# A four-layer graph network on one core: last weights turned by VectorE from blocks, the attention-to-mean stretch reordered, denominators' chain in three parts

## The reference

```python
x = _layernorm(x + relu(adj @ (bin(x) @ sign(w0).T)))                 # binary layer
# attention layer: type sums, gates, masked exp scores, normalized sum
e = jnp.where(adj != 0, jnp.exp(-leaky_relu(s_left[:, None] + s_right[None, :], 0.01)), 0.0)
attn = e / (jnp.sum(e, axis=1, keepdims=True) + 1e-05)
x = _layernorm(x + sigmoid(attn_a * (attn @ h) + attn_b * (adj @ (x @ W_gcnb) + b_gcnb)))
# mean layer
A = (adj != 0)
x = _layernorm(x + A @ (x @ W + b) / jnp.sum(A, axis=0)[:, None])
# two GAT layers
for l in range(2):
    Wh, Ws = jnp.split(y @ W_stack[l], 2, axis=-1)
    a = softmax(Wh @ Ws.T, axis=-1) * adj
    y = leaky_relu(a @ Wh + y, 0.01)
```

## Time and profile before

| | us |
|---|---|
| median of 3 runs | 476.89 |
| lowest, highest | 476.69, 477.68 |
| the profiled execution, whole | 477.23 |
| its span, first to last instruction | 475.4 |
| PE busy | 463.0 |
| DVE busy | 372.1 |
| ACT busy | 232.3 |
| POOL busy | 190.6 |

### The profile page before, as it was taken

One profiled execution on the slowest core, in us unless ns is written; L12 is line 12 of the kernel. 1 busy time (PEld: TensorE's weight loads), 2 busy tenths in 40 slices (PEclk: granted clock), 3 DMA queues, 4 the chain that ended last, 5 costly groups with the idle time before them and its releaser, 6 DMA issues.

```text
span 475.4 us, 5636 instructions
## 1 busy us (share of the span) xinstructions
PE 463.0 (97%) x1854; PEld 304.2 (64%) x1854; DVE 372.1 (78%) x832; ACT 232.3 (49%) x411; POOL 190.6 (40%) x186
## 2 busy tenths in 40 slices
PE   8999999999999999999999999899999999999993
PEld 6999745545555588877544444454557546778882
DVE  4688799999998599739236757998755698799984
ACT  5979529980889653323334532251332475342200
POOL 1444665631425058823001541361430064456641
PEclk9999999999999999999999999999999999999999
DMA  8856310000364100000000000000000000000001
GB/s 280 284 181 193 123 40 0 1 1 0 117 193 161 32 0 1 0 1 1 1 0 0 0 1 1 1 0 1 0 1 0 1 1 1 0 13 22 23 22 40
DMA packets 8180, 20.68 MB, mean 44 GB/s; under 512 B 1008, under 2 KB 4740, under 8 KB 8152
## 3 DMA queue, kind: packets, MB, share of 16 engines
q1 hardware_dynamic: 7144, 19.02, 12.3%
q0 software_dynamic: 464, 0.79, 0.7%
q10 hardware_dynamic: 544, 0.52, 0.3%
HBM read 18.94 MB, written 1.39 MB: 43 GB/s over the span
## 4 chain that ended last, share of the span: by engine, by line
PE 87%; DVE 7%; issue 2%; DMA 2%; SPq 1%; ACT 1%; POOLq 0%; POOL 0%; DVEq 0%
PE psum L1544 19%; PE psum L1359 11%; PE psum L1335 11%; PE psum L1581 9%; PE psum L1644 8%; PE psum L1316 6%; PE psum L1422 6%; PE psum L1524 4%; PE psum L1237 2%; PE psum L1497 2%; PE psum L1379 2%; PE psum L1615 2%; PE psum L1406 2%; DMA adj_rows<-in_adj_dram 2%; PE psum L1476 1%
## 5 line engine op out<-in xcount | busy, mean ns | idle before, releaser
L1544 PE MATMUL psum<-QT,xT 128*128 128x512 f32 (+3 forms) x264 | 108.3, 542 | 1.7 <-ACT ST L634 1.7
L440 POOL TENSOR_TENSOR es<-es,ST 128x512 f32<-128x512 f32 (+3 forms) x60 | 74.9, 1248 | 53.8 <-ACT ST L639 52.1
L634 ACT ACTIVATE ST<-psum 128x512 f32<-128x512 f32 (+3 forms) x66 | 36.1, 546 | 89.6 <-DVE rm L994 77.9
L1544 PEld LDWEIGHTS psum<-QT,xT 128*128 128x128 f32 (+1 forms) x264 | 48.1, 186 | 44.5 <-issue 38.2
L994 DVE TENSOR_TENSOR rm<-psum,rm 128x512 f32<-128x512 f32 (+3 forms) x60 | 37.4, 624 | 41.2 <-PE psum L1544 41.0
L376 POOL TENSOR_TENSOR rstd<-veps,nhalf 128x1 f32<-128x1 f32 (+1 forms) x44 | 29.4, 668 | 65.0 <-DVE veps L770 65.0
L1644 PE MATMUL psum<-Wh,ST 128*128 128x256 f32 (+3 forms) x242 | 55.1, 380 | 0.0
L1581 PE MATMUL psum<-ST,Wh 128*128 128x512 f32 (+3 forms) x132 | 53.9, 542 | 0.0
L404 POOL TENSOR_TENSOR esumb<-esumb,eb 128x1354 f32<-128x1354 f32 (+1 forms) x10 | 34.5, 3447 | 46.4 <-ACT eb L528 46.4
L1359 PE MATMUL psum<-eb,x_all 128*128 128x512 f32 (+3 forms) x132 | 51.8, 542 | 0.0
L1335 PE MATMUL psum<-adjT,x_all 128*128 128x512 f32 (+3 forms) x132 | 50.1, 542 | 0.0
(11 more groups left out here) (181 smaller groups left out, 781.7 us busy)
## 6 DMA issues: line engine op xcount, KB each, us to landing
adj_rows<-in_adj_dram SPq DMA_DIRECT2D x10, 677.0 KB, 5.2
rows<-in_adj_dram SPq DMA_DIRECT2D x10, 677.0 KB, 4.0
x_all<-in_x_dram SPq DMA_DIRECT2D x5, 256.0 KB, 4.5
out_dram<-xs SPq DMA_DIRECT2D x10, 128.0 KB, 1.7
W<-in_L_gnn_W_stack_dram SPq DMA_DIRECT2D x2, 512.0 KB, 6.4
adj_rows<-in_adj_dram SPq DMA_DIRECT2D x1, 338.5 KB
rows<-in_adj_dram SPq DMA_DIRECT2D x1, 338.5 KB
...
```

Source lines behind the costliest of these rows:

```text
L440: nc.gpsimd.tensor_tensor(es[0:r, g % 2, 0:w], es[0:r, g % 2, 0:w], buf(g)[0:r, j, 0:w], ALU.add)\
L1544: last = nc.tensor.matmul(psum[0:r, SB[n % 3], 0:w], xT[l][:, k, j * P:j * P + r], QT[:, k, c0:c1], start=(k == 0), stop=(k == KD - 1))
```

## The change

On SP, `load_blocks(l)` is new: four DMAs of 32x32x32 elements for each of the two layers of `W_stack`, in runs of 32 floats, so that 32x32 blocks stand where a block-wise turn on DVE makes the whole of `W3T`. On DVE, `turn_w3(l)` does that turn; PE's 16 turns and ACT's four copies are gone. On PE, `turn_exps(0)` stands inside `h_part(9)`, `turn_exps(1)` before `h_part(10)`, `turn_exps(2)` and `h_proj(0)` inside it. `low_half` goes from POOL to DVE, four of eleven masks (3, 6, 8, 10) from DVE to ACT (a Sign and a Square each), `row_degree(0)` comes ahead of `exp_scores(6)`. The degrees' reciprocals come after the first tiles on DVE instead of ahead of `coef`. In the GAT layers, `den_blocks` is cut into `den_turn`, `den_gather` and `den_spread`, and at the first turn alone they stand after s = 1, 3 and 5; `scale_t(0)` goes from s = 0 to s = 6, `add_t` from 2 to 7, `leaky_t` from 3 to 8.

```diff
+    ACT_MASKS = [3, 6, 8, 10]
...
-        W3T = at("W3T", at_e + 3 * LONG + 6 * D, [P, 2, KD, D])
+        W3B = [at("W3B0", at_e, [P, 2 * KD, D]), at("W3B1", at_e + LONG, [P, 2 * KD, D])]
+        W3T = [at("W3T0", at_w, [P, 2, KD, D]), at("W3T1", at_e + 2 * LONG, [P, 2, KD, D])]
...
+            def load_blocks(l):
+                sp.wait_ge(h_step.sem, RING + l + 1)
+                sp.wait_ge(den_added.sem, RING + l + 1)
+                for a in range(QUADS):
+                    sp.dma_start(W3B[l][a * BLOCK:(a + 1) * BLOCK, :, :].rearrange("u e (b v) -> u e b v", v=BLOCK),
+                                 w3[l].rearrange("(b u) (e a v) -> a u e b v", u=BLOCK, a=QUADS, v=BLOCK)[a]).then_inc(w3b_in[l].sem, 16)
+
             sp.wait_ge(agga_done.sem, T)
             for i in range(T):
+                if i >= T - 2:
+                    load_blocks(i - T + 2)
                 if i >= 2:
                     sp.wait_ge(deg_ready.sem, T + i - 1)
...
-            rsqrt(NB, 0)
             for i in range(T):
-                if i + 1 < T:
-                    rsqrt(NB, i + 1)
-                low_half(i)
+                rsqrt(NB, i)
+                if i >= LAG:
+                    add_bias2(i - LAG)
+            for i in range(T - LAG, T):
                 add_bias2(i)
...
-            i = 0
             exp_scores(RING - 1)
+            row_degree(0)
+            i = 1
             for j in range(RING, T):
                 exp_scores(j)
-                for _ in range(2 if i + T - j < T else 1):
+                for _ in range(2):
                     if i < T:
                         row_degree(i)
                         i += 1
...
+            def mask_sign(j):
+                r = kk(j)
+                if j >= MASKS:
+                    act.wait_ge(c_step.sem, j - MASKS + 1)
+                own.link(nc.scalar.activation(maskT[j % MASKS][0:r, 0:N], adjT[0:r, j, 0:N], ACT.Sign))
+
+            def mask_square(j):
+                r = kk(j)
+                nc.scalar.activation(maskT[j % MASKS][0:r, 0:N], maskT[j % MASKS][0:r, 0:N], ACT.Square).then_inc(mask_ready_act.sem, 1)
+
+            mask_sign(3)
+            mask_square(3)
             for c, (c0, c1) in enumerate(CH):
...
+            for i in range(2, T):
+                high_half(i)
+                if i + 2 < T:
+                    gate(i + 2)
+                if i in (2, 4, 6):
+                    mask_sign(i + 4)
+                if i in (3, 5, 7):
+                    mask_square(i + 3)
+                scale_b2(i)
...
+            def turn_w3(l):
+                dve.wait_ge(w3b_in[l].sem, 16 * QUADS)
+                if l == 1:
+                    dve.wait_ge(h_step.sem, RING + 3)
+                    dve.wait_ge(den_added.sem, RING + 3)
+                nc.vector.transpose(W3T[l][:, :, :, :].rearrange("p h e n -> p (h e n)"), W3B[l][:, :, :].rearrange("p e n -> p (e n)"))\
+                    .then_inc(w3T_ready.sem, 1)
...
+            turn_w3(0)
             den_sums(0)
+            turn_w3(1)
+            den_sums(1)
             dve.wait_ge(att_t_ready.sem, 1)
...
-            for i in range(T):
+            for i in range(2, T):
+                norm_apply(NB, i, vbuf[0:kk(i), i % 4, :])
+                if i + 2 < T:
+                    attn_sum(i + 2)
                 if i + 1 < T:
                     attn_out(i + 1)
-                norm_apply(NB, i, vbuf[0:kk(i), i % 4, :])
-                if i + 3 < T:
-                    attn_sum(i + 3)
-                if i + 4 < T:
-                    mean_mask(i + 4)
+                low_half(i)
+                if i + 2 < T:
+                    mean_mask(i + 2)
...
-                den_blocks(g)
+                if g > 0:
+                    den_turn(g)
+                    den_gather(g)
+                    den_spread(g)
                 for s in range(last):
                     both(g + 1, s)
-                    if s == 0:
+                    if g == 0 and s == 1:
+                        den_turn(g)
+                    if g == 0 and s == 3:
+                        den_gather(g)
+                    if g == 0 and s == 5:
+                        den_spread(g)
+                    if s == add - 1:
                         scale_t(g)
...
-            turnover(0, T, 2)
+            turnover(0, T, 7)
...
             def mul_w3(l):
-                pe.wait_ge(w3T_ready.sem, 2 * l + 2)
-                if l == 1:
-                    pe.wait_ge(m3_ready.sem, 1)
+                pe.wait_ge(w3T_ready.sem, l + 1)
+                pe.wait_ge(hT_ready.sem, KD + 1 + l)
```

164 lines of the change are left out of this document (80 added, 84 removed).

## The result

| | before | after |
|---|---|---|
| median, us | 476.98 (4 runs) | 480.91 (4 runs, 478.85 to 481.14) |
| the profiled execution, whole | 477.23 | 478.85 |
| its span | 475.4 | 477.0 |

The changed kernel takes 1.0062 times as long as the kernel before (95% interval 1.0042 to 1.0082; the two medians alone would give 1.0082). It is slower where 473.4 was forecast, outside the range that was given.

What follows compares the result with a forecast made beforehand. PE was taken as the bound, busy 463.0 of 475.4 us. Gains of 1.97 (weight turns) and 1.6 (chain), 3.6 taken as 3.5, bring the median from 476.89 to 473.4; range 472.8 to 478.5.

Steps and rivals of the forecast that it cites:

- The turns of the weights: Between the projections and first c_part: two rows of eight turns and a wait for W3T leave PE, 1.97 us gained.
- The block loads: SP's loads ahead of the last two row loads: 16 ns per 128-byte run assumed, so no cost to PE.
- The slack of 0.7 us: Before h_proj(0): hT's second copy done at 162.8, PE wants it at 163.5; gone at 17.4 ns per run.
- The first rival: Block loads late and kernel slower: at 32 ns per run net +4.0 us, 480.9; chance 0.17.
- PE hides both; nothing gained, nothing lost: In the c_part steps: DVE's load under 3.2 us and ACT's about 2.4 fit PE's 3.34 us; no gain or loss.
- something else slower, such as a wait in the c_part steps: A rival for any other slowdown, with no size given; chance 0.02.
- The chain in three parts: At the turn from GAT step 0 to 1: PE's 1.71 us wait for PSUM goes, 1.6 us gained.
- The margin of 0.2 us: At sum_t(1,9): PE wants its tile at about 323.7 and gets it at about 323.5; 0.1 us taken off.
- the turn's gain is not kept: DVE, 3.3 us later against PE, makes PE wait in sum_t(1,j) or the next turn: 474.9; chance 0.13.

Runs made afterwards that it cites:

- e6: The kernel of e1 with the turn from GAT step 0 to 1 put back as in the kernel before; 475.32 us, ratio 0.9961.
- e7: The kernel of e1 with the same block-load bytes in 4 KB runs instead of 128 bytes, so two layers use wrong weights; 474.16 us, ratio 0.9936.
- e8: The kernel of e1 with each of the eight block loads cut in two, in runs of 64 bytes instead of 128; 484.38 us, ratio 1.0140.
- e1: The changed kernel with GpSimd's last seven bias additions waiting until VectorE has made the last low half; 474.78 us, ratio 0.9946.
- e3: The kernel before with only the edit at the turn from GAT step 0 to 1 (denominators' chain in three parts); 476.32 us, ratio 0.9977.
- e11: The changed kernel with GpSimd's additions from tile 5 on each waiting for the one before to finish; 474.75 us, ratio 0.9944.
- e5: The kernel of e1 with den_turn(0) ahead of the first maximum of GAT step 2's scores instead of behind s = 1; 473.45 us, ratio 0.9917.

## Where the prediction was right and where it failed

**The turns of the weights, 1.97 us: right.** The first `c_part` starts at 172.55, where 172.8 was forecast, 2.24 us ahead of the earlier trace rows. PE was 0.17 us later going in (154.51 for 154.34), so the stretch gave 2.4 us. e6 gives 1.9 for the whole part, with 0.4 us of waiting for `hT` in it.

**The block loads: right that short runs cost, a little low.** The run of 128 bytes was taken at 16 ns, the middle of two far bounds, and is 11 to 15 by e7; that it was so near is partly luck. Row load 10 was to land at 156.1, and ACT started on it at 157.20. The sum ran on the DMA engines' time alone and left out SP, which issued the two sets in 3.3 and 3.8 us and had the row load behind them in its queue. The profiled execution had just no wait for `hT`; other kernels had 0.3 to 0.8 us. The slack of 0.7 us was real and gone, the cost 0 to 0.8 us. The first rival had its threshold at t = 24 ns; e8 shows the loss behind it.

**"PE hides both; nothing gained, nothing lost": here it failed.** This step, on the low halves, the masks and the order of the `c_parts`, summed the busy time of DVE in a step and held it against PE's 3.34 us. For the full steps that is right: the `c_parts` run without a gap from 172.55 on. It didn't ask what the edit leaves behind on POOL, and the edit's own lines had it: `LAG = 7` and a last loop with seven `add_bias2` and nothing in between. It also read the earlier trace rows one-sidedly. That `L949` takes 0.96 us beside POOL's low half and 0.41 later was taken as time that comes back. It is a row on two engines holding each other up, and so a price for each instruction of DVE that stands beside POOL's. For `norm_apply` the bound is the length of POOL's unbroken work, and the trace of the kernel before had a case of it, the 1.51 us beside two instructions, with the very instruction that then took 4.94. At 0.69 us for each addition, seven could have been priced at 4.9. What the runs showed in place of "nothing lost" is 3.1 us of waiting and 1.7 us by the clock, 6.1 us in the medians (e1). The rival "something else slower, such as a wait in the c_part steps" had the right place, but no mechanism, no price and a chance of 0.02.

**The chain in three parts, 1.6 of 1.71 us: mechanism right, size wrong.** The wait at the turn is gone. What was to be late next, `sum_t(1,9)`, was named and given 0.1 us, and this is the term that was mis-sized: it and one place in the next turn took 1.1 us back, 0.5 to 1.0 us stayed (e3, e1 against e6). The margin of 0.2 us there came from a DVE schedule with no gap in 26 us, where every instruction beside POOL can be longer than in its own row. The rival "the turn's gain is not kept" gave 474.9, and the kernel without the stall, e1, is at 474.78. That it fits so well is partly luck, since some of the turn's gain was kept and up to 0.8 us went into the wait for `hT`. So even with the failed step right, the forecast of 473.4 would have been 1.4 us too low.

**The sum.** In the profiled execution: -2.2 for the turns, +3.1 for the stall, +1.7 for the clock, -0.6 for the turn of the steps, together +2.0 against a span that grew by 1.6. The range had nothing of this kind in it: it was built from the cost of the block loads alone.

## What to carry to other kernels

When work moves off an engine, look at what remains there: instructions that had been kept apart now follow one another, and an unbroken row on GpSimd can shut an instruction of VectorE out for its whole length, as it did `norm_apply` here. Put such a row where no instruction on the critical chain stands beside it, or break it with a wait (e1 and e11, 6 us each for one line). When a wait goes, the engine that had its idle time there is the next to be late; give it its work in that idle time (e5), and price a margin of tenths of a microsecond as gone. A VectorE instruction that is *busy* for longer than its shape needs, beside a row of GpSimd, is a wait in disguise: look for such rows before the change.
